# Tiles kept over the seams of attention, preparation and mixing, and q computed by tokens

## The chip, the cores and the metric

The kernel runs on one core of one Trainium2 chip. The metric is the device time of one execution in microseconds (us); several executions are given with their median. The core has five engines that run their own instruction queues: TensorE (PE in the rows, PEld its weight loads), VectorE (DVE), ScalarE (ACT), GpSimd (POOL) and SyncE (SP), which here issues nearly all DMA transfers. They wait for each other by semaphores.

## The reference

Four sequences of 512 tokens and 512 channels go through four residual layers. The change lies in the first (cross attention, 16 heads of 128, RMS norm on q and k) and at the start of the two that follow it in the kernel:

```python
q = (hidden_states @ Wq).reshape(B, Sq, H, D)
k = (encoder_hidden_states @ Wk).reshape(B, Skv, H, D)
v = (encoder_hidden_states @ Wv).reshape(B, Skv, H, D)
q = rmsnorm(q, gq)
k = rmsnorm(k, gk)
scores = jnp.einsum('bqhd,bkhd->bhqk', q, k) * scale
attn = jax.nn.softmax(scores, axis=-1)
out = jnp.einsum('bhqk,bkhd->bqhd', attn, v).reshape(B, Sq, H * D)
return out @ Wo

x = x + attention(layernorm(x), ctx_1024, ...)
x = x + hadamard_ffn(layernorm(x), ...)      # fwht, gate and up, silu(gate) * up, fwht, down
x = x + ssm(ctx_1024, layernorm(x), ...)     # in_proj, convolution, silu, low rank, softplus, scan
x = x + mixture_of_experts(layernorm(x), ...)
```

## The kernel before

It is written engine by engine: each stage is a block in which every engine has its own program, and what is written there is the order in which it runs. A `Scope` ends with a barrier of all engines and gives its tiles back. Matrix products are made of pairs of rounded parts: `split_product` gives three products, high x high, high x low and low x high (L99 to L101); so every result that is used in a product again is copied as its high part by ScalarE and subtracted as its low part by VectorE.

**Attention** (`stage_attention`) runs 32 iterations: 8 pairs of heads, hp, times 4 sequences, b; i = 4 hp + b, j = i + 1. Work of iteration i (scores, exp, transposed probabilities, attention product, projection) is woven with K, q and V of iteration j. Banks of PSUM: `ps_s` (scores), `ps_pt` (transposed probabilities), `ps_w` (three banks for K, q, V and the projection), `ps_o` (the attention product). K is computed by tokens, 128 at a time, for both heads (256 columns), copied to `kn`, squared by GpSimd, summed and scaled per token, and turned by transposes against the identity (`turn_k`, L365). q is computed by channels, already turned: `queries`, 12 products of 512 columns for each head. ScalarE makes its high part (L550) and its square (L551, `qsq`); the sum over the channels lies across partitions, so `sums_q` makes it with 8 products of `qsq` and a column of ones into `ps_o` (L371); GpSimd raises the result to -1/2 (L680), and `exp` takes it as a scale. On TensorE, the second half of an iteration reads: the first head's attention product, `turn_k` for both heads, `turn_p(1, 0)` and `turn_p(1, 1)` (L385, transposed probabilities of the second head), V's first half (`kv`), `turn_p(1, 2)`, `sums_q`, `turn_p(1, 3)`, V's second half, then the second head's attention product `pv(i, 1)`, which waits for VectorE's subtraction behind `turn_p(1, 3)` (L801). On VectorE: L781 (q low), L806 (the attention product's low part), L786 (K low), L801, L797 (q sums), L801. ScalarE splits a half of an expert's weights (L577) once per iteration; SP loads the context, expert weights, xn and ffn weights ahead.

**Preparation** (`stage_prep`): loads the in-projection, constants and the first context tiles, turns the in-projection (L1170) and the down weights (L1137), normalizes and turns four rows of x (`norm`, `turn`, `norm_out`), with the standard deviation by three Newton steps on VectorE. Then 16 steps of channel products (`channels`), a convolution of four taps on VectorE (L1437, L1440), rotation of the down weights, step sizes. GpSimd does the butterflies.

**Mixing** (`stage_mix`): 64 blocks, in which TensorE makes gate, up and down products and VectorE and GpSimd run the state recurrence: drive (L1918), decay (L1772, ScalarE), scan (L1989). SP loads delta, du, rows and, through three buffers, gate and up weights `gu` of 1 MB per block.

## Time and profile before

| | us |
|---|---|
| median of 3 runs | 2483.26 (2483.11 to 2485.51) |
| profiled execution | 2479.53 |
| its span | 2477.7 |
| TensorE busy | 2260.7 |
| VectorE busy | 1768.8 |
| GpSimd busy | 1366.2 |
| ScalarE busy | 1291.6 |

The span is the time from the first to the last instruction of the program that was profiled. Attention runs to about 1212 us, preparation to about 1351, mixing to about 2060, router and experts to the end. Busy times are unions over instructions; a TensorE row's duration is longer than its share, since products overlap: the distance of two starts tells what one costs. An idle time before an instruction is shown in brackets with what ended it; short ones are left out.

### The profile page before, as it was taken

What the parts mean: (1) busy time and instruction counts of PE and PEld (TensorE: products, weight loads), DVE (VectorE), ACT (ScalarE), POOL (GpSimd) and SP (SyncE); (2) the same over time, 40 slices, a digit from 0 to 9 for tenths busy, and PEclk for the clock granted to TensorE, in tenths of its full rate; (3) what the DMA queues carried; (4) which work ended last, traced back from release to release, by engine and by line L of the source; (5) the groups of instructions that cost most, each with busy time, mean ns of one, the idle gap of its engine ahead of it and who ended that gap; (6) DMA issues with size and microseconds to landing.
All of it is one profiled execution on the core that took longest, in us unless ns stands there. A gap on an engine that the chain in (4) does not pass through costs nothing. (4 is left out here: it accounts for less than half of the span.)

```text
span 2477.7 us, 31987 instructions
## 1 busy us (share of the span) xinstructions
PE 2260.7 (91%) x10784; PEld 1745.7 (70%) x10784; DVE 1768.8 (71%) x3390; ACT 1291.6 (52%) x2246; POOL 1366.2 (55%) x1107
## 2 busy tenths in 40 slices
PE   5899999999999999999695899899899986999994
PEld 4788888888888888888551666566566554777773
DVE  7676776777677676766585898898898996634344
ACT  3555555554555555555475766766766653223331
POOL 2444444444444444444185887997998993233331
PEclk9999999999999999999897999999999997899997
DMA  7655555464645545452446766565565532369865
GB/s 298 239 192 197 183 183 200 154 217 170 218 161 194 193 172 206 158 204 107 161 139 232 250 190 208 166 209 180 174 206 176 188 107 89 120 225 347 335 216 194
DMA packets 148066, 480.77 MB, mean 194 GB/s; under 512 B 24577, under 2 KB 61697, under 8 KB 124481
## 3 DMA queue, kind: packets, MB, share of 16 engines
q1 hardware_dynamic: 138208, 449.78, 51.7%
q0 software_dynamic: 7520, 24.74, 2.8%
q10 hardware_dynamic: 2176, 4.19, 0.4%
q8 instruction: 90, 1.47, 0.2%
q14 instruction: 72, 0.58, 0.1%
HBM read 361.19 MB, written 117.47 MB: 193 GB/s over the span
## 5 line engine op out<-in xcount | busy, mean ns | idle before, releaser
L671 POOL TENSOR_SCALAR att_probs<-att_probs,att_recip 128x512 f32<-128x512 f32 x256 | 179.2, 703 | 377.3 <-DVE att_recip L765 377.3
L1918 POOL TENSOR_TENSOR mix_drive<-mix_du,mix_rows 128x512 f32<-128x512 f32 x256 | 326.5, 1282 | 36.8 <-DMA mix_rows<-bc_d 9.4
L1989 DVE TENSOR_TENSOR_SCAN mix_state<-mix_state,mix_drive 128x512 f32<-128x512 f32 x256 | 312.9, 1222 | 42.4 <-POOL mix_drive L1918 30.1
L563 ACT ACTIVATE att_probs<-att_s,att_bias,att_rq 128x512 f32<-128x512 f32 x256 | 199.9, 781 | 226.9 <-DVE att_bias L761 226.6
L1772 ACT ACTIVATE mix_state<-mix_delta,mix_a 128x512 f32<-128x512 f32 x256 | 175.9, 690 | 217.8 <-DVE mix_drive L2000 188.0
L1903 POOL TENSOR_TENSOR mix_y<-mix_y,mix_drive 128x512 f32<-128x512 f32 x180 | 230.7, 1282 | 46.5 <-DVE mix_drive L2000 46.3
L1682 PE MATMUL mix_down<-mix_wd,mix_hT 128*128 128x512 f32 x512 | 233.9, 600 | 7.7 <-DVE residual_x L2020 7.7
L569 ACT CAST att_pT<-att_pt 128x512 fp32r<-128x512 f32 x256 | 143.6, 591 | 174.1 <-PE att_pt L385 169.5
L760 DVE TENSOR_REDUCE att_nmax<-att_s 128x1 f32<-128x512 f32 x256 | 174.8, 683 | 62.8 <-PE att_s L101 62.7
L801 DVE TENSOR_TENSOR att_pT<-att_pt,att_pT 128x512 fp32r<-128x512 f32 x256 | 170.1, 685 | 65.0 <-ACT att_pT L569 58.3
L1682 PEld LDWEIGHTS mix_down<-mix_wd,mix_hT 128*128 128x128 f32 x512 | 98.1, 192 | 110.1 <-issue 96.1
L99 PE MATMUL att_w<-att_w_qkv,att_cx 128*128 128x256 f32 x512 | 155.5, 304 | 0.2 <-POOL att_w_qkv L707 0.2
L385 PE MATMUL att_pt<-att_ident,att_probs 128*128 128x128 f32 x1024 | 141.8, 276 | 10.9 <-DVE att_pT L801 5.9
L101 PE MATMUL att_w<-att_w_qkv,att_cx 128*128 128x256 f32 x512 | 150.6, 294 | 0.0
L100 PE MATMUL att_w<-att_w_qkv,att_cx 128*128 128x256 f32 x512 | 150.4, 294 | 0.0
L680 POOL TENSOR_TENSOR att_rq<-att_qss,att_power 128x8 f32<-128x8 f32 x32 | 55.1, 1723 | 165.6 <-DVE att_qss L797 165.6
L697 POOL TENSOR_TENSOR att_expert_w<-att_expert_w 128x1536 fp32r<-128x1536 f32 x32 | 112.1, 3502 | 61.5 <-DVE att_w_qkv L747 34.2
L385 PEld LDWEIGHTS att_pt<-att_ident,att_probs 128*128 128x128 f32 x1024 | 118.2, 143 | 27.0 <-DVE att_pT L801 17.1
L2704 POOL DMA_INDIRECT parts<-exp_y,exp_target x47 | 49.2, 1048 | 152.9 <-ACT exp_y L2741 86.4
L2000 DVE TENSOR_TENSOR mix_drive<-mix_state,mix_rows 128x512 f32<-128x512 f32 x180 | 124.4, 691 | 6.2
L806 DVE TENSOR_TENSOR att_oT<-att_o,att_oT 128x512 fp32r<-128x512 f32 x64 | 44.2, 691 | 103.1 <-ACT att_oT L581 102.9
L812 DVE TENSOR_TENSOR residual_x<-att_w,residual_x 128x512 f32<-128x512 f32 x128 | 85.3, 686 | 37.1 <-PE att_w L101 37.1
(384 smaller groups left out, 6670.8 us busy)
## 6 DMA issues: line engine op xcount, KB each, us to landing
mix_gu<-guT SPq DMA_DIRECT2D x64, 1024.0 KB, 8.3
att_xn<-normT SPq DMA_DIRECT2D x31, 2048.0 KB, 8.6
split_w<-att_expert_w SPq DMA_DIRECT2D x32, 1536.0 KB, 6.4
lead_w<-split_w SPq DMA_DIRECT2D x16, 3072.0 KB, 12.1
mix_rows<-bc_d SPq DMA_DIRECT2D x128, 256.0 KB, 5.0
att_cx<-ctxT SPq DMA_DIRECT2D x30, 1024.0 KB, 8.6
guT<-att_ffnT SPq DMA_DIRECT2D x32, 512.0 KB, 6.1
mix_wd<-wdT SPq DMA_DIRECT2D x16, 1024.0 KB, 7.9
```

The source lines that it names most:

```text
L99: pe.matmul(out, lh, rh, start=start, stop=False)
L101: return pe.matmul(out, ll, rh, start=False, stop=stop)
L385: tr = pe.transpose(ps_pt[(b + n) % 2][:, t, :], probs[:, h * TB + t, k * P:(k + 1) * P], ident_sb[:, :])
L563: act.activation(probs[:, n, :], ps_s[n % 2][:, :], ACT.Exp, bias=bias[:, n:n + 1], scale=rq[:, n:n + 1], accum_out=sums[:, n:n + 1]).then ...
L671: pool.tensor_scalar(probs[:, n, :], probs[:, n, :], recip[:, n:n + 1], 1.0, ALU.mult, ALU.mult).then_inc(s_pn, 1)
L760: own.after(dve.tensor_reduce(nmax[:, n:n + 1], ps_s[n % 2][:, :], AX_X, ALU.max, negate=True))
L801: dve.tensor_tensor(pT[:, 1, k, :], ps_pt[(b + (TB + 1) * h + k) % 2][:, :, :].rearrange("p t n -> p (t n)"), pT[:, 0, k, :].bitcast(F32), ...
L1682: mm = pe.matmul(ps_y[:, :], hT[c % 2][:, k, tok], wd[c % 2][:, k, :], start=(k == 0), stop=(k == CHUNK - 1))
L1772: act.activation(state[q % BANKS][:, :], delta[i % DELTAS][:, :], ACT.Exp, scale=a[:, t, n:n + 1]).then_inc(s_decay, 1)
L1903: pool.tensor_tensor(out[:, :], out[:, :], drive[q % RING][:, :], ALU.add).then_inc(s_padd, 1)
L1918: pool.tensor_tensor(drive[q % RING][:, :], du[i % DUS][:, :], rows[g % ROWS][:, 0, :], ALU.mult).then_inc(s_drive, 1)
L1989: dve.tensor_tensor_scan(h[:, :], h[:, :], drive[q % RING][:, :], 0.0, ALU.mult, ALU.add).then_inc(s_scan, 1)
```

## The change

**q by tokens.** `queries` now works like `kv`: 128 tokens at a time, both heads, 256 columns, 48 products in place of 24. ScalarE copies q to a new tile `qn`, GpSimd squares it (`square_q`, in K's tile of squares), VectorE sums it (`sum_q`, now a reduction of 1024 elements per partition and a small one), and TensorE turns it (`turn_q`, 8 transposes) into the banks it came from; ScalarE and VectorE then make the parts. `sums_q`, the column of ones and the squares on ScalarE are gone.

```diff
+                def queries(half, bank):
+                    for a in range(2):
+                        t = 2 * half + a
+                        rows = slice(t * P, (t + 1) * P)
+                        for k in range(KD):
+                            mm = split_product(pe, ps_w[bank][:, a * W2:(a + 1) * W2],
+                                               (xn[:, 0, k, rows], xn[:, 1, k, rows]),
+                                               (wpart(0, "q", k), wpart(1, "q", k)), k == 0, k == KD - 1)
                     mm.then_inc(s_q, 1)
+
+                def turn_q(j, h, bank):
+                    pe.wait_ge(s_qc, 2 * j + 2)
+                    for t in range(TB):
+                        tr = pe.transpose(ps_w[bank][:, t * P:(t + 1) * P], qn[:, t, h, :], ident_sb[:, :])
+                    tr.then_inc(s_qt, 1)
...
                         turn_k(0, 1)
-                        pe.wait_ge(s_qlo, 2 * j + 1)
-                        turn_k(1, 2)
+                        turn_q(j, 0, 2)
                     turn_p(i, b, 1, 0)
                     turn_p(i, b, 1, 1)
                     if not last:
+                        turn_q(j, 1, 0)
+                        pe.wait_ge(s_qlo, 2 * j + 1)
+                        turn_k(1, 2)
+                    turn_p(i, b, 1, 2)
+                    if not last:
                         pe.wait_ge(s_qlo, 2 * j + 2)
                         kv(cx, "v", 0, 0, s_v)
-                    turn_p(i, b, 1, 2)
-                    pe.wait_ge(s_olo, 2 * i + 3)
-                    if not last:
-                        pe.wait_ge(s_qsq, 2 * j + 2)
-                        sums_q()
                     turn_p(i, b, 1, 3)
                     if not last:
                         pe.wait_ge(s_ktlo, 2 * j + 1)
                         kv(cx, "v", 1, 1, s_v)
-                        pe.wait_ge(s_qss, j + 1)
+                    pe.wait_ge(s_olo, 2 * i + 3)
                     pv(i, 1)
...
+                def square_q(j):
+                    pool.wait_ge(s_qc, 2 * j + 2)
+                    pool.wait_ge(s_kss, j + 1)
+                    pool.tensor_tensor(ksq[:, :, :, :], qn[:, :, :, :], qn[:, :, :, :], ALU.mult).then_inc(s_qsq, 1)
...
+                def sum_q(own, j):
+                    dve.wait_ge(s_qsq, j + 1)
+                    own.after(dve.tensor_reduce(qss[:, :], ksq[:, :, :, :].rearrange("p t h d -> p h t d"), AX_X, ALU.add))
+                    dve.tensor_scalar(qss[:, :], qss[:, :], 1.0 / D, RMS_EPS, ALU.mult, ALU.add).then_inc(s_qss, 1)
```

**Tiles over the seams.** A class `Bridge` takes the place of `Scales` and is allocated before attention. It holds the identity and Hadamard matrices, all small constants of preparation and mixing, a tile `raw` (attention's raw weights, then the in-projection, later the turned rows of mixing) and two tiles `gu`, which serve as context tiles in attention and preparation and then as the first two gate and up tiles of mixing.

```diff
+                    if b == B - 1 and 1 <= hp:
+                        for to, src in strided[hp - 1::PAIRS - 1]:
+                            sp.dma_start(to, src, allow_slow_non_contiguous=True).then_inc(s_strided, 16)
+                    if b == 1 and hp == PAIRS - 1:
+                        sp.wait_ge(s_w, 2 * PAIRS)
+                        sp.dma_start(raw[:, 0:ET * CD].rearrange("p (t d) -> p t d", t=ET),
+                                     in_proj.rearrange("(t p) d -> p t d", p=P)).then_inc(s_inproj, 16)
...
+                def load_gu(i):
+                    sp.wait_ge(s_x, ET * (B - 1 + i))
+                    sp.dma_start(bridge.gu[i][:, :, :, :, :].bitcast(F32), guT[i]).then_inc(s_gu, 16)
...
                 load_rows(0)
-                load_gu(0)
                 for i in range(1, ET):
                     load_delta(i)
                     load_du(i)
-                load_gu(1)
                 load_rows(1)
```

In preparation the in-projection, the identity and the first two contexts are there at the start; `norm`, `turn` and `norm_out` of the four rows move into the first four steps of the loop; GpSimd's power replaces the Newton steps; the signed Hadamard matrices (8 instructions, L1412 and L1413) move from the start to just ahead of the first convolution, and the statistics behind the scaling of the down weights:

```diff
+                input_lo(0)
+                input_lo(1)
+                dve.wait_ge(s_dsc, 1)
+                scale_down(0)
                 spread()
...
+                down_lo(0)
+                shifts()
+                down_lo(1)
                 signed_hadamard()
...
+                    if s < TB:
+                        norm(s)
                     if s < B * ET:
                         u(s // ET, s % ET)
```

How the order moves. TensorE in the second half of an attention iteration, before (kn is K by tokens, probs the probabilities, w_qkv with cx the V products):

```order
L365 MATMUL att_w<-att_ident,att_kn 128x128 x8
L385 MATMUL att_pt<-att_ident,att_probs 128x128 x8
L99 MATMUL att_w<-att_w_qkv,att_cx 128x256
...
L385 MATMUL att_pt<-att_ident,att_probs 128x128 x4
L371 MATMUL att_o<-att_ones,att_qsq 128x1 x8
```

and in the change, at the same place:

```order
L369 MATMUL att_w<-bridge_ident,att_kn 128x128 x4
L364 MATMUL att_w<-bridge_ident,att_qn 128x128 x4
L383 MATMUL att_pt<-bridge_ident,att_probs 128x128 x8
L364 MATMUL att_w<-bridge_ident,att_qn 128x128 x4
L369 MATMUL att_w<-bridge_ident,att_kn 128x128 x4
L383 MATMUL att_pt<-bridge_ident,att_probs 128x128 x4
L99 MATMUL att_w<-att_w_qkv,bridge_gu 128x256
```

The V products now stand behind seven groups of four transposes, and the products with ones are gone.

VectorE at the same place, before (oT is the attention product's low part, pT the probabilities' low part):

```order
L776 TENSOR_SCALAR att_kn<-att_kn,att_rk 128x128 x8
L781 TENSOR_TENSOR att_qT<-att_w,att_qT 128x512
L806 TENSOR_TENSOR att_oT<-att_o,att_oT 128x512
L786 SCALAR_TENSOR_TENSOR att_kT<-att_w,att_gain,att_kT 128x512 x2
L801 TENSOR_TENSOR att_pT<-att_pt,att_pT 128x512 x3
L797 TENSOR_SCALAR att_qss<-att_o 128x8
```

and in the change:

```order
L791 TENSOR_SCALAR att_kn<-att_kn,att_rk 128x128 x8
L822 TENSOR_TENSOR att_oT<-att_o,att_oT 128x512
L801 SCALAR_TENSOR_TENSOR att_kT<-att_w,att_gain,att_kT 128x512
L796 TENSOR_TENSOR att_qT<-att_w,att_qT 128x512
L817 TENSOR_TENSOR att_pT<-att_pt,att_pT 128x512 x2
L796 TENSOR_TENSOR att_qT<-att_w,att_qT 128x512
L801 SCALAR_TENSOR_TENSOR att_kT<-att_w,att_gain,att_kT 128x512
L812 TENSOR_REDUCE att_qss<-att_ksq 128x8
```

Both subtractions of q and the reduction of its squares now stand behind the attention product's.

## Rows read from the trace of the kernel before

**Rows 1.** Stretches (attention, mixing): us, busy PE, PEld, DVE, ACT, POOL, PEclk, DMA, GB/s.
```profile
77.00:1212.00 1135.00, 1115.84 (x6364) 956.47 (x6364) 799.25 (x1767) 597.58 (x1192) 508.36 (x437) 0.98 0.50 181
...
1363.00:2045.00 682.00, 634.06 (x2216) 413.88 (x2216) 609.96 (x720) 448.88 (x615) 606.99 (x485) 0.98 0.57 187
```

**Rows 2.** L577 up to 1180 us: count, duration ns min/median/max, first and last start.
```profile
L577 ACT CAST att_expert_w<-att_expert_w x31: 1474/1477/1484, 94.0 to 1169.4; 128x1536 fp32r<-128x1536 f32 x31
```

**Rows 3.** Timeline of TensorE in one iteration: start us, us, engine, line, op, count.
```profile
625.51 1.03 PE L365 MATMUL att_w<-att_ident,att_kn 128*128 128x128 f32 x8
...
628.99 0.66 PE L385 MATMUL att_pt<-att_ident,att_probs 128*128 128x128 f32 x4
629.49 1.84 PE L371 MATMUL att_o<-att_ones,att_qsq 128*128 128x1 f32 x16
631.19 0.64 PE L385 MATMUL att_pt<-att_ident,att_probs 128*128 128x128 f32 x4
...
633.32 0.48 PE L99 MATMUL att_o<-att_pT,att_v 128*128 128x512 f32 x1
...
660.92 1.04 PE L365 MATMUL att_w<-att_ident,att_kn 128*128 128x128 f32 x8
```

**Rows 4.** Timeline of VectorE in the same iteration, with the idle time before.
```profile
616.05 1.22 DVE L769 TENSOR_REDUCE att_kss<-att_ksq 128x8 f32<-128x1024 f32 x1 [1.18 <-POOL att_ksq L667]
...
626.33 0.69 DVE L806 TENSOR_TENSOR att_oT<-att_o,att_oT 128x512 fp32r<-128x512 f32 x1 [0.36 <-ACT att_oT L581]
626.94 1.40 DVE L786 SCALAR_TENSOR_TENSOR att_kT<-att_w,att_gain,att_kT 128x512 fp32r<-128x512 f32 x2
628.26 1.28 DVE L801 TENSOR_TENSOR att_pT<-att_pt,att_pT 128x512 fp32r<-128x512 f32 x2
...
632.48 0.69 DVE L801 TENSOR_TENSOR att_pT<-att_pt,att_pT 128x512 fp32r<-128x512 f32 x1 [0.95 <-ACT att_pT L569]
```

**Rows 5.** Timeline of ScalarE, the copy of the last transposed probabilities.
```profile
631.86 0.59 ACT L569 CAST att_pT<-att_pt 128x512 fp32r<-128x512 f32 x1 [1.59 <-PE att_pt L385]
```

**Rows 6.** Timeline of TensorE: twelve products of 256 columns, then twelve of 512.
```profile
609.27 0.28 PE L99 MATMUL att_w<-att_w_qkv,att_cx 128*128 128x256 f32 x1
...
610.73 0.50 PE L99 MATMUL att_s<-att_kT,att_qT 128*128 128x512 f32 x1
...
613.67 0.39 PE L99 MATMUL att_w<-att_xn,att_w_qkv 128*128 128x512 f32 x1
...
616.39 1.03 PE L385 MATMUL att_pt<-att_ident,att_probs 128*128 128x128 f32 x8
```

**Rows 7.** Timeline of TensorE, an iteration in which the clock falls.
```profile
1166.59 1.84 PE L371 MATMUL att_o<-att_ones,att_qsq 128*128 128x1 f32 x16
...
1169.03 0.41 PE L101 MATMUL att_w<-att_w_qkv,att_cx 128*128 128x256 f32 x1
```

**Rows 8.** Timelines of VectorE, then TensorE, at the start of the preparation stage.
```profile
1213.15 2.47 DVE L1395 BATCH_NORM_STATS2 prep_stats<-residual_x 128x6 f32<-128x512 f32 x4 [1.31 <-PEq L75]
...
1219.28 0.28 DVE L1412 TENSOR_SCALAR first_hs<-prep_had_f,prep_su 128x128 f32<-128x128 f32 x1
...
1221.97 1.28 DVE L1407 TENSOR_SCALAR prep_wraw<-prep_wraw,prep_dsc 128x2048 f32<-128x2048 f32 x1
...
1235.11 0.75 DVE L1437 TENSOR_SCALAR prep_conv<-prep_x,prep_taps 128x512 f32<-128x512 f32 x1 [0.47 <-PE prep_x L101]
...
1216.73 1.11 PE L1170 MATMUL prep_dbl_ps<-first_ident,prep_relu 128*128 128x128 f32 x4 [5.62 <-DMA first_ident<-in_ident]
...
1232.95 0.78 PE L99 MATMUL prep_x<-prep_cx,prep_inT 128*128 128x512 f32 x1
```

**Rows 9.** Timelines of GpSimd, TensorE and VectorE at the start of the mixing stage.
```profile
1360.70 1.26 POOL L1918 TENSOR_TENSOR mix_drive<-mix_du,mix_rows 128x512 f32<-128x512 f32 x1 [9.41 <-DMA mix_rows<-bc_d]
...
1363.31 0.80 PE L99 MATMUL mix_gate<-first_uT,mix_gu 128*128 128x512 f32 x1 [25.93 <-DMA mix_gu<-guT]
...
1370.76 1.23 DVE L1989 TENSOR_TENSOR_SCAN mix_state<-mix_state,mix_drive 128x512 f32<-128x512 f32 x1 [2.76 <-ACT mix_state L1772]
```

More of the change, by code:

```diff
@@ L101, in split_product, with stage_attention @@
     return pe.matmul(out, ll, rh, start=False, stop=stop)
[L104 to L119 removed]
+def stage_attention(nc, xs, x, ctx, xT, ctxT, Wq, Wk, Wv, Wo, gq, gk, W_gate, W_up, guT, Wg, Wu, Wd, split_w, ident, in_proj, bridge, strided):
     D = P
@@ L331, in _ @@
                 sp.wait_ge(s_est, 16 * PAIRS * B)
+                sp.wait_ge(s_strided, 16 * len(strided))
+                sp.wait_ge(s_inproj, 16)
+                for i in range(2):
+                    sp.wait_ge(s_cx[i], 16 * PAIRS * B // 2)
                 sp.wait_ge(s_fst, 16 * (PAIRS * B + 1))
@@ L366, in turn_k @@
                     tr.then_inc(s_kt, 1)
-                def sums_q():
-                    for n in range(HP * TB):
-                        h, t = divmod(n, TB)
-                        mm = pe.matmul(ps_o[:, n:n + 1], qsq[:, h, t * P:(t + 1) * P], ones[:, :], start=True, stop=True)
-                    mm.then_inc(s_ss, 1)
                 def turn_p(i, b, h, k):
@@ L648, in iteration @@
                         kt_hi(j, 0)
+                        q_hi(j, 0)
+                    pt_hi(i, b, 1, 0)
+                    pt_hi(i, b, 1, 1)
+                    if not last:
+                        q_hi(j, 1)
                         kt_hi(j, 1)
-                    for k in range(TB):
-                        pt_hi(i, b, 1, k)
+                    pt_hi(i, b, 1, 2)
+                    pt_hi(i, b, 1, 3)
                     expert_hi(i)
@@ L734, in iteration @@
                     norm_p(i, 7)
+                    if not last:
+                        square_q(j)
                     split_ffn(i)
@@ L908, in iteration @@
                     pt_lo(i, b, 0, 3)
-                    if not last:
-                        q_lo(j, 0)
                     row_recip(i, 7)
@@ L1493, with stage_mix @@
 EXPERTS = 16
[L1496 to L1498 removed]
+def stage_mix(nc, xs, uT0, hs, guT, wdT, bridge, u_d, delta_d, du_d, bc_d):
+    BLOCKS = bridge.sud.shape[1]
     ALL = B * BLOCKS
```

244 lines of the change are left out of this document (106 added, 138 removed).

## Prediction

> **What bounds the kernel now.** I read the stretches by stage first, then the timeline of one attention iteration on each engine, then the two seams. The attention stage fills nearly half of the span, and in it TensorE is busy 1115.8 of 1135 us; no other engine is above 800 us [rows 1]. So the stage lasts as long as TensorE's row of work plus its waits. The reader is to see in [rows 2] that 31 L577 starts, one per iteration, lie between 94.0 and 1169.4 us: 35.85 us each. An iteration in which nothing disturbs the clock is shorter: from one first L365 to the next, 660.92 - 625.51 = 35.41 us [rows 3]. The rest, 30 x 0.44 = 13 us, is the clock: in some iterations, right behind the one-column products of L371, TensorE goes from 2.4 to 1.2 GHz: the 256-column product takes 0.41 us there and 0.28 elsewhere [rows 6, 7], and the stage's granted clock is 0.98 [rows 1]. Such an iteration is 1.1 to 1.2 us longer, so there are about 12 of them.
>
> The stretch that the change rewrites runs from L365 (start of the K transposes, 625.51) to the second head's attention product (633.32): 7.81 us [rows 3]. Call its start 0. In it TensorE already waits: twice, for 0.2 to 0.3 us, for VectorE's subtractions. VectorE is the chain behind it: L806 at 0.82, two L786 from 1.43, two L801 from 2.75 to 4.03, and the last L801 at 6.97 [rows 4].
>
> The mixing stage is the second long one: TensorE 634 of 682 us, VectorE 610, GpSimd 607 [rows 1]. They are coupled in the order of the blocks, so it moves as a whole with its start.
>
> **The change part by part. First, q by tokens.**
> (1) Removed on TensorE: 8 one-column products per iteration, L371 from 629.49 to the next row at 631.19, 1.70 us [rows 3].
> (2) Added on TensorE: 8 transposes of q. Eight K transposes take 0.87 us [the start of row L365 in rows 3 to the next group], or 0.1 us each; so 0.8 us.
> (3) Changed: 24 products of 512 columns become 48 of 256. Twelve of the first kind last 616.39 - 613.67 = 2.72 us, so 0.227 each; twelve of the second 610.73 - 609.27 = 1.46, so 0.12 each [rows 6]. 48 x 0.12 - 24 x 0.227 = +0.3 us. It lies in a part of the iteration where TensorE waits for nobody, so it counts in full.
> By work alone this would be -1.70 + 0.8 + 0.3 = -0.6 us per iteration.
>
> (4) But TensorE gets three new places to wait at, all on VectorE. I walk through the stretch. TensorE now has K head 0, q head 0, two groups of probabilities, q head 1: 20 transposes, done at 2.05. The next row (K head 1) writes the bank of q head 0, and waits for its subtraction. VectorE now does L806 at 0.82, one K subtraction at 1.43 (0.66), the q subtraction at 2.09 (same shape as L806, 0.69 long), done at 2.78 [durations from rows 4]. TensorE waits some 0.8 us. Then VectorE has two probability subtractions (0.6 each) and q head 1's, done at 2.69 + 3 x 0.61 + 0.1 = 4.6. The first half of the V products writes that bank, so it starts at 4.7, not at 1.7 as now; behind it in TensorE's queue stands the last transpose of probabilities. 12 x 0.12 plus 0.08 for the switch puts that at 6.22; now it is at 5.68 (631.19) [rows 3]. From there to the attention product it is ScalarE's copy 0.67 later, VectorE's subtraction 0.62 after that, its 0.69 and 0.15 more: 2.13 us [rows 3 to 5]. So the product starts at 8.35 in place of 7.81: **+0.54 us**. In that time VectorE also has the K head 1 subtraction (0.66) and the new sum of q squares: a reduction of 1024 elements per partition, like L769's 1.22 us, plus a small one [rows 4]. It is free at 7.14 and is needed at 7.5, so it hides, with 0.36 us to spare.
> Bounds of this term. Below: VectorE's rows of the new stretch add up to 7.0 us back to back (0.61 x 6 + 0.66 x 2 + 1.34 + 0.69), from 0.82; the product can't start before 7.95, so it is at least +0.14. Above: each of the three waits may bring 0.1 us of wake-up more, and the reduction may outlast its cover by 0.3: +0.85. I take 0.54, since every step has a row of the same shape. All that comes behind the attention product is TensorE's row, so it passes the loss on.
> (5) ScalarE loses two squarings and gets no more than it loses; GpSimd gets a square of 1024 elements behind its last normalization, in a gap before the ffn split. ScalarE and GpSimd are busy 598 and 508 of 1135 us [rows 1], so at nothing; if it weren't covered, GpSimd's 1.9 us would delay the q sum and show in (4).
> (6) SP: ten small strided loads and in_proj's go before the expert load, one or two per pair of heads, and two context loads at the end. Expert halves and xn have most of an iteration; at nothing.
> So an iteration gets longer by 0.54 + 0.3 = 0.84, and 31 have it: **+26 us** (bounds 0.44 and 1.15: +14 and +36).
>
> (7) The clock. With the ones products the known cause of the falls is gone. But from 0 to 4.7 TensorE now does nothing but 28 transposes and waits; today the longest run without a wide product goes from 628.99 to the four transposes at 631.19 and their 0.4 us, 2.6 us [rows 3]. I put the falls at 16 instead of 12, **+5 us**; bounds: none left (-13) and one in every iteration (+23).
> The Trainium skill (TensorE: Matmul & The Clock Gate, "Why this matters for your kernels") wants only that the engine has no long idle gaps between bursts; the falls in [rows 7] come without any, so here row and rule differ. By that rule neither version would fall, and the sum would be 13 us lower. Part 4 of the same page, on PE-mode transposes, says that these do not count as busy for the clock; by it the new stretch of transposes is worse than today's, which is the last rival below.
>
> **Second, the seam from attention to preparation.** Now the stage begins at 1213.15 (VectorE); TensorE waits until 1216.73 for the identity matrix, turns weights and the first normed rows by turns, and comes to the first channel product at 1232.95; the first convolution starts at 1235.11 [rows 8]. With matrices resident, I walk it anew from 1213.2 at the same low clock: turn 1.1, copy 0.6, subtract 0.7, twice: 1218.1. VectorE scales the down weights (1.28 us [rows 8]; their load now stands first in the queue, and I take it as landed by 1218.5) until 1219.8. VectorE then has the statistics, 2.47 us [rows 8] and 0.7 for small ones, before its subtraction, which ends at 1223.6. Two rotations of 512 columns (0.43 each at 1.2 GHz) and a turn (0.9) put the first channel product at 1225.4, 7.5 us earlier. Behind it the signed Hadamard, 8 instructions 0.2 us apart (0.28 each [rows 8]), now stands just ahead of the first convolution: 1228.7, **-6.4 us**. The normalizations of four rows and their turns go into the loop, into ScalarE's and TensorE's idle time; not covered, they would cost 4 x 1 us. Bounds -3 and -8. VectorE's convolutions pace the stage, so its end moves along.
>
> **Third, the seam to mixing.** GpSimd starts at 1360.70 on the rows, TensorE at 1363.31 on gate weights; they and the second block's (1 MB each) stand in the load queue between the first chunk's rows and the other chunks. The third scan on VectorE, 1370.76, waits 2.76 us for ScalarE [rows 9], whose decay stands in its order behind the sigmoid of that late gate. With both weight blocks there, gate and up of block 0 are done before the rows come, and du and delta 1 have 1 MB less ahead of them (5.6 us at the stage's 187 GB/s [rows 1]; I take 4, since a burst runs above a mean). The third scan goes from 1370.76 to about 1365: **-5.8 us**. Bounds -3 (only the queue's part) and -9 (the rows come earlier too).
>
> **Sum**: +26 + 5 - 6.4 - 5.8 = **+19 us** on the profiled execution's 2479.5, 2498.5; the median of the runs is 3.7 above that execution, so 2502.
>
> **The rivals.**
> A. *Faster, the walk is wrong and TensorE's work decides*: if the three waits do not arise, (1) to (3) give 31 x -0.6 = -18, the seams -12, the falls up to -13: 2440 to 2453. For it: TensorE is busy 98% of the stage. Against: VectorE's own 7.0 us don't fit into a stretch of 7.2. It decides from where the q subtractions end before 2.1 and 3.5. Chance 0.12.
> B. *The falls vanish with the ones products*, the walk holds: 26 - 13 - 12 = +1, 2484. Chance 0.17.
> C. *Waits at their lower bound or seams at their upper*: 14 + 5 - 17 = +2, down to -10 with fewer falls: 2473 to 2486. Chance 0.13.
> D. *The clock falls in each iteration*: +26 + 23 - 12 = +37, 2520. For it: 4.7 us with transposes only. Chance 0.15.
> E. *The seams don't pay* (the loads just come late elsewhere, the rows pace the mix's start as before): +31, 2514. Chance 0.05.
> My forecast, with falls between 8 and 22, has 0.38, and reaches from 2490 to 2514.
>
> **How the numbers follow.** The time is the forecast's, 2502. The range has it with B, C, D and E for the most part: 2470 to 2522; A is left out. A measurement of this kernel can tell about 0.2%, 5 us. Faster by more: A, a third of C and of B: 0.22. Within: the rest of these two, 0.15. Slower: 0.63.
>
> **What would show it.** In the profile after: L371 gone; TensorE's wait for the q subtraction (VectorE) ahead of the K head 1 turn, about 0.8 us, and another of 0.8 ahead of the first V product; 8.3 to 8.4 us from the K turn to the attention product; L577's successor 36.2 us apart in an undisturbed iteration, and 37.4 where the clock fell. The first channel product some 12 us behind the stage's start (now 20), the third scan of mixing some 14 us behind its start (now 19.6). It would be wrong if iterations came out at 34.8, or if granted clock in attention went to 1.00 or under 0.95 (now 0.98 [rows 1]).

## The result, and the profile after

The changed kernel takes **2547.61 us** (median of 4 runs, 2541.56 to 2548.3), the kernel before 2483.35 us in runs beside it (2483.11 to 2485.51). The ratio is 1.0251, 95% interval 1.0236 to 1.0266: 64 us slower, where I had forecast 19 slower and a range that ended at 2522. The profiled execution took 2547.45 us, its span is 2544.8.

First the stretches of the profile after that answer to [rows 1] (columns as there), attention and then mixing:

```profile
77.00:1287.00 1210.00, 1115.61 (x6847) 972.89 (x6844) 912.75 (x1796) 607.96 (x1190) 565.24 (x469) 0.98 0.48 171
1421.00:2105.00 684.00, 634.04 (x2205) 413.81 (x2206) 607.53 (x717) 451.40 (x619) 603.23 (x483) 0.97 0.57 187
```

Mixing is as it was. Attention is 75 us longer and TensorE's busy time in it the same 1116 us, so what came in is waiting. VectorE, with 29 instructions more, is busy 113 us more. That is too much for 31 sums of 1.4 us (43 us); the rest lies in one line of the program, the scaling of K, below. The expert copies of ScalarE, one per iteration, answer to [rows 2]; they are now (1243.5 - 93.8) / 30 = 38.32 us apart, and 38.10 where nothing disturbs the clock:

```profile
L575 ACT CAST att_expert_w<-att_expert_w x31: 1475/1480/1486, 93.8 to 1243.5; 128x1536 fp32r<-128x1536 f32 x31
```

Next, what TensorE waited for in attention (us in total, times, longest), after and then before, where the view's longest entries are single events:

```profile
PE att_w L369 <- DVE att_kn L791: 55.3, 29, 1.9
PE att_w L99 <- DVE att_qT L796: 12.2, 23, 0.6
PE att_w L369 <- DVE att_qT L796: 7.1, 17, 0.4
```
```profile
PE att_pt L385 <- DVE att_pT L801: 3.2, 2, 2.1
PE att_s L99 <- ACT att_probs L563: 1.3, 1, 1.3
```

The two waits for q (L796) are the ones that I had forecast. The one at the top is not in my sum at all: the turn of K head 0 waits 1.9 us for the scaling of K, which the change doesn't touch. Here are VectorE, GpSimd and TensorE in one iteration of after:

```profile
617.34 5.06 DVE L791 TENSOR_SCALAR att_kn<-att_kn,att_rk 128x128 f32<-128x128 f32 x8
...
617.52 0.76 POOL L683 TENSOR_SCALAR att_probs<-att_probs,att_recip 128x512 f32<-128x512 f32 x1 [0.41 <-DVE att_recip L780]
...
618.25 1.89 POOL L679 TENSOR_TENSOR att_ksq<-att_qn 128x1024 f32<-128x1024 f32 x1
...
620.12 0.61 POOL L698 TENSOR_SCALAR att_ffnT<-att_ffn_raw 128x512 fp32r<-128x512 f32 x1
...
620.81 1.30 POOL L700 TENSOR_TENSOR att_ffnT<-att_ffn_raw,att_ffnT 128x512 fp32r<-128x512 f32 x1
...
622.45 0.66 PE L369 MATMUL att_w<-bridge_ident,att_kn 128*128 128x128 f32 x4 [1.91 <-DVE att_kn L791]
```

VectorE's eight scalings take 5.06 us from start to end. Before, in the iteration of [rows 3], they took 2.36:

```profile
623.01 2.36 DVE L776 TENSOR_SCALAR att_kn<-att_kn,att_rk 128x128 f32<-128x128 f32 x8
```

One scaling is usually 0.28 us long. The view of the tile gives count, shortest, median and longest in ns, before and then after:

```profile
L776 DVE TENSOR_SCALAR att_kn<-att_kn,att_rk x256: 267/276/648, 39.2 to 1162.2; 128x128 f32<-128x128 f32 x128
```
```profile
L791 DVE TENSOR_SCALAR att_kn<-att_kn,att_rk x256: 267/282/1950, 39.4 to 1235.1; 128x128 f32<-128x128 f32 x128
```

The longest is 1.95 us, and GpSimd's new square beside it is 1.89 us. Laid beside GpSimd's rows, four of the eight are stretched: one of 0.64 us that runs until the last normalization ends, one of 1.95 beside the square, one of 0.67 beside the first half of the ffn split (0.61) and one of 1.28 beside its second half (1.30). GpSimd's instruction has begun first each time, and the stretched scaling ends some 0.08 us behind its end, in all 124 cases of this trace. Between the two halves of the split one scaling of the usual length gets through. So VectorE's instruction lasts as long as what is left of GpSimd's. The kernel before shows the same in small: its longest scaling, 648 ns against a median of 276, stands beside a normalization of 0.77, and in all 31 iterations one scaling is stretched so beside the normalization and one beside the first half of the split (0.67).

### The profile page after: what moved, and what is told of

Same layout as the page of the kernel before. It is cut to its first block and busy times, and to the rows that moved or that the text cites. A ratio compares the mean times of both kernels' runs of the same rounds, so it can differ in the third digit from the quotient of the medians.

```text
span 2544.8 us, 33092 instructions
## 1 busy us (share of the span) xinstructions
PE 2267.4 (89%) x11296; PEld 1766.2 (69%) x11296; DVE 1883.2 (74%) x3407; ACT 1302.7 (51%) x2246; POOL 1425.0 (56%) x1141
## 5 line engine op out<-in xcount | busy, mean ns | idle before, releaser
L99 PE MATMUL att_w<-att_w_qkv,bridge_gu 128*128 128x256 f32 x512 | 150.4, 294 | 13.1 <-DVE att_qT L796 12.8
L791 DVE TENSOR_SCALAR att_kn<-att_kn,att_rk 128x128 f32<-128x128 f32 x256 | 158.4, 691 | 0.2 <-POOL att_rk L688 0.2
L383 PE MATMUL att_pt<-bridge_ident,att_probs 128*128 128x128 f32 x1024 | 150.4, 289 | 2.2 <-DVE att_pT L817 1.1
L99 PE MATMUL att_w<-att_w_qkv,att_xn 128*128 128x256 f32 x512 | 148.0, 289 | 0.0
L100 PE MATMUL att_w<-att_w_qkv,att_xn 128*128 128x256 f32 x512 | 145.3, 284 | 0.0
L101 PE MATMUL att_w<-att_w_qkv,att_xn 128*128 128x256 f32 x512 | 145.3, 284 | 0.0
L100 PE MATMUL att_w<-att_w_qkv,bridge_gu 128*128 128x256 f32 x512 | 144.0, 281 | 0.0
L101 PE MATMUL att_w<-att_w_qkv,bridge_gu 128*128 128x256 f32 x512 | 143.9, 281 | 0.0
L2707 POOL DMA_INDIRECT parts<-exp_y,exp_target x47 | 49.3, 1048 | 152.8 <-ACT exp_y L2744 101.9
```

Source lines behind the costliest of these rows:

```text
L99: pe.matmul(out, lh, rh, start=start, stop=False)
L100: pe.matmul(out, lh, rl, start=False, stop=False)
L101: return pe.matmul(out, ll, rh, start=False, stop=stop)
```

## The experiments

**1. The square behind the scalings** (late_square), the changed kernel with one wait more. GpSimd works in the order of its program, so the split of the ffn piece moves behind the scalings too:

```diff
                 def square_q(j):
                     pool.wait_ge(s_qc, 2 * j + 2)
                     pool.wait_ge(s_kss, j + 1)
+                    pool.wait_ge(s_kn, j + 1)
```

> The changed kernel with one wait more: GpSimd's square of q starts only when VectorE's eight scalings of K are done. Theory (the two engines take turns at something both need): in the changed kernel one of the eight scalings of every iteration lasts 1,950 ns, as long as the square of 1,890 ns beside it, two more last 0.67 and 1.28 us beside GpSimd's split of the ffn piece (0.61 and 1.30 us), the eight take 5.06 us in place of 2.36, and TensorE waits 1.91 us for them. With the square behind the scalings, and the split behind the square, the eight should take about 2.0 us, TensorE's wait for them should be gone (at most 0.2 us), and the undisturbed iteration should fall from 38.1 to about 36.2 us: 31 x 1.9 = 59 us, so 2,547 - 59 = 2,488 us (2,480 to 2,500, by how often the granted clock falls). Rival (the scalings are late for another reason, say their order in VectorE's queue, and the long scaling only looks like the square's): the eight still take about 5 us and the time stays at 2,540 to 2,550. Second rival (what the square does beside the scalings it then does beside the K parts, the q parts or V): the eight are short, but VectorE's subtractions behind them become longer by as much, and less than 20 us come back.

Measured: 2477.06 us (10 runs, ratio to before 0.9968, interval 0.9954 to 0.9982), and 2477.68 (12 runs) when it ran once more below. 70 us are gone, more than I expected. The scalings, their longest, the square and TensorE's next row in its trace:

```profile
587.74 1.99 DVE L792 TENSOR_SCALAR att_kn<-att_kn,att_rk 128x128 f32<-128x128 f32 x8
...
589.91 1.89 POOL L680 TENSOR_TENSOR att_ksq<-att_qn 128x1024 f32<-128x1024 f32 x1 [1.23 <-DVE att_kn L792]
...
590.81 0.60 PE L369 MATMUL att_w<-bridge_ident,att_kn 128*128 128x128 f32 x4
...
592.48 1.28 POOL L701 TENSOR_TENSOR att_ffnT<-att_ffn_raw,att_ffnT 128x512 fp32r<-128x512 f32 x1
...
592.89 0.68 DVE L797 TENSOR_TENSOR att_qT<-att_w,att_qT 128x512 fp32r<-128x512 f32 x1
```

1.99 us for the eight, no wait on TensorE. And the subtractions that now stand beside GpSimd's work, as the last row, are no longer than elsewhere (0.68 us); one of their operands lies in PSUM. So the second rival falls too. Between two L575 starts an undisturbed iteration is 36.03 us in place of 38.10: 31 x 2.07 = 64 us. The other 7 are the clock (experiment 7).

**2. The same work, needless, in the kernel before** (spare_square), where GpSimd squares the K squares in place once more:

```diff
+                def square_again():
+                    pool.tensor_tensor(ksq[:, :, :, :], ksq[:, :, :, :], ksq[:, :, :, :], ALU.mult)
...
                     norm_p(i, 7)
+                    if not last:
+                        square_again()
                     split_ffn(i)
```

> The kernel before with one instruction more in each iteration and nothing else changed: GpSimd squares the 1,024 elements of the K squares once more, in place, at the spot where the change puts the square of q (behind the eighth normalization, ahead of the split of the ffn piece). Nobody reads the result and nobody waits for it. Theory: the eight scalings of K go from 2.36 to about 5 us as in the changed kernel, TensorE's K turns start 2.0 to 2.6 us later, and with them the iteration is 37.4 to 38.0 us in place of 35.4: 31 x (2.0 to 2.6) = 62 to 81 us, so 2,545 to 2,564 us. Rival (an idle GpSimd does this work free, as the prediction had it): 2,483 to 2,490 us, scalings at 2.36.

Measured: 2577.26 us, ratio 1.0374 (1.0357 to 1.0391): 93 us for an instruction nobody waits for.

```profile
627.08 5.06 DVE L781 TENSOR_SCALAR att_kn<-att_kn,att_rk 128x128 f32<-128x128 f32 x8
...
627.99 1.90 POOL L670 TENSOR_TENSOR att_ksq<-att_ksq 128x1024 f32<-128x1024 f32 x1
...
632.20 1.11 PE L365 MATMUL att_w<-att_ident,att_kn 128*128 128x128 f32 x4 [2.47 <-DVE att_kn L781]
```

The 5.06 us to the hundredth. The undisturbed iteration is 38.01 us, 2.60 longer than before, so 81 us, the end of what I expected; the time lies above it. The profiled execution was 2561.73 us, 78 over the median of before; the other four, at a mean granted clock of 0.948 to 0.951 against its 0.955, were 9 to 18 us longer. That more falls of the clock make up this rest is argued, not shown.

**3. The control** (spare_late), the same spare square started behind the scalings:

```diff
                     if not last:
+                        pool.wait_ge(s_kn, j + 1)
                         square_again()
```

> The control for the spare square: the kernel before with the same needless GpSimd square of 1,024 elements in every iteration, but started only when VectorE's eight scalings of K are done. The amount of work on every engine is that of the run with the spare square, only its place differs. Theory (place, not amount: the two engines take turns only where both work from and to SBUF): the eight scalings take about 2.0 us, TensorE waits for none of them, 2,483 to 2,490 us. Rival (the iteration is longer because GpSimd has 1.9 us more work, wherever it lies): 2,540 us or more.

Measured: 2487.14 us, ratio 1.0008 (0.9989 to 1.0027), no difference. The scalings take 2.00 us, and TensorE's K turns have no wait before them:

```profile
626.02 2.00 DVE L782 TENSOR_SCALAR att_kn<-att_kn,att_rk 128x128 f32<-128x128 f32 x8
...
628.10 1.90 POOL L670 TENSOR_TENSOR att_ksq<-att_ksq 128x1024 f32<-128x1024 f32 x1 [1.14 <-DVE att_kn L782]
...
628.46 1.04 PE L365 MATMUL att_w<-att_ident,att_kn 128*128 128x128 f32 x8
```

Its square starts 2.08 us behind the first scaling's start (628.10 against 626.02), in the run before 0.91 (627.99 against 627.08). GpSimd's 1.9 us more per iteration cost nothing in the one place and 93 us in the other, 1.2 us earlier. It is the place.

**4. Half the square** (half_square); the sums for half of the tokens of q are left wrong:

```diff
-                    pool.tensor_tensor(ksq[:, :, :, :], qn[:, :, :, :], qn[:, :, :, :], ALU.mult)
+                    pool.tensor_tensor(ksq[:, 0:2, :, :], qn[:, 0:2, :, :], qn[:, 0:2, :, :], ALU.mult)
```

> The changed kernel, but GpSimd squares only the first half of q (512 of 1,024 elements a partition; the sums of the other half are left wrong, so the output isn't the reference's). Nothing else is changed. Theory: one scaling of K lasts as long as the square beside it, so with a square of about 0.95 to 1.0 us in place of 1.89 the longest of the eight should last about 1.0 us in place of 1.95, the eight about 4.1 in place of 5.06, and the iteration should be 0.9 us shorter: 31 x 0.9 = 28 us, 2,519 us (2,512 to 2,526). Rival (a fixed cost of every change of engine, whatever the length): the same 2,547 within 4 us. Rival (the scalings are only slowed in proportion while both run): also less than the full 0.9 us, 2,530 to 2,540.

Measured: 2510.31 us, ratio 1.0104 (1.0084 to 1.0125), 37 us less than the changed kernel.

```profile
639.43 4.22 DVE L791 TENSOR_SCALAR att_kn<-att_kn,att_rk 128x128 f32<-128x128 f32 x8
...
640.34 1.03 POOL L679 TENSOR_TENSOR att_ksq<-att_qn 128x512 f32<-128x512 f32 x1
...
643.71 0.66 PE L369 MATMUL att_w<-bridge_ident,att_kn 128*128 128x128 f32 x4 [1.06 <-DVE att_kn L791]
```

The square is 0.86 us shorter, the eight scalings 0.84, TensorE's wait 0.85, the iteration 0.86 (37.24). One for one: neither a fixed cost for each meeting nor a mere slowing in proportion. 31 x 0.86 = 27; of the other 10 us some 7 are the clock, which no longer falls in the loop (experiment 7), and the rest stays open.

**5. The square on ScalarE** (scalar_square):

```diff
                     ffn_out(i, b)
+                    if not last:
+                        act.wait_ge(s_qc, 2 * j + 2)
+                        act.wait_ge(s_kss, j + 1)
+                        act.activation(ksq[:, :, :, :], qn[:, :, :, :], ACT.Square).then_inc(s_qsq, 1)
```

> The changed kernel with the square of q on ScalarE, one Square of 1,024 elements from the SBUF copy, put in ScalarE's idle 2.1 us between its copy of the ffn piece and its copy of the attention product; no wait is added. GpSimd does as much as before the change. Theory: ScalarE beside the scalings costs them nothing, but GpSimd's split of the ffn piece (0.61 and 1.30 us) still falls among them, so the eight take about 3.7 us (2.0 + 0.4 + 1.3), TensorE waits 0 to 0.5 us for them, and the iteration is 36.0 to 36.6 us: 2,474 to 2,492 us. Rival (the scalings suffer from any other engine that reads SBUF): 5 us again and 2,540 us or more.

Measured: 2488.15 us, ratio 1.0013 (0.9995 to 1.0031). ScalarE reads and writes the same tiles as GpSimd did, beside the same scalings:

```profile
627.40 3.39 DVE L791 TENSOR_SCALAR att_kn<-att_kn,att_rk 128x128 f32<-128x128 f32 x8
```
```profile
628.42 1.07 ACT L550 ACTIVATE att_ksq<-att_qn 128x1024 f32<-128x1024 f32 x1
...
628.62 0.67 POOL L701 TENSOR_SCALAR att_ffnT<-att_ffn_raw 128x512 fp32r<-128x512 f32 x1 [0.28 <-ACT att_ffn_raw L576]
...
629.37 1.33 POOL L703 TENSOR_TENSOR att_ffnT<-att_ffn_raw,att_ffnT 128x512 fp32r<-128x512 f32 x1
```

The longest scaling here is 1.31 us, as GpSimd's last row, and GpSimd's two rows explain the whole: what the eight take over the 1.99 of late_square, 1.4 us, is less than the two (0.67 + 1.33), and nothing is left for ScalarE's 1.07. TensorE waits 0.24 us for the scalings, and the iteration is 36.43: 31 x 0.40 = 12 us over late_square, where 11 were measured. This also parts the 2.07 us of experiment 1: 38.10 - 36.43 = 1.67 us per iteration are the square, the other 0.40 the two rows of the split that stay beside the scalings here.

**6. The seams alone** (seams_only), the q part undone:

> The changed kernel with the q part undone: q, its squares and its sums by products with ones as in the kernel before, and only the tiles kept over the seams (weights, transposed context, gate and up weights, identity, the small vectors) with the new order of the preparation. In the changed kernel the stretch from the start of the preparation to the end is about 7.3 us shorter than before. Theory (the two halves of the change are independent): attention takes as long as before, and the total is 2,483 - 7 = 2,476 us (2,471 to 2,480). The prediction had 12 us for this half: 2,471. Rival (the kept tiles or the loads put among the last iterations of attention cost something there): 2,480 to 2,490, with longer iterations where the loads stand.

Measured: 2477.25 us, ratio 0.9971 (0.9955 to 0.9986): 7 us faster, 4 to 11. Attention is as before (its stage ends at the same 1213). So the q part by itself costs some 71 us, and the seams give 7 back. Preparation starts with (TensorE and VectorE of after, answering to [rows 8]):

```profile
1287.58 0.63 PE L1179 MATMUL prep_dbl_ps<-bridge_ident,bridge_raw 128*128 128x128 f32 x4 [2.05 <-PEq L75]
...
1299.76 0.78 PE L99 MATMUL prep_x<-bridge_gu,prep_inT 128*128 128x512 f32 x1
```
```profile
1293.04 1.29 DVE L1415 TENSOR_SCALAR prep_wraw<-prep_wraw,prep_dsc 128x2048 f32<-128x2048 f32 x1 [1.42 <-DMA prep_wraw<-in_L_ffn_W_down]
...
1302.93 0.74 DVE L1442 TENSOR_SCALAR prep_conv<-prep_x,bridge_taps 128x512 f32<-128x512 f32 x1
```

The first channel product comes 12.2 us behind the stage's start (19.8 before), the first convolution 15.4 (22.0 before). The third scan of mixing, and what it waits for:

```profile
1436.73 1.23 DVE L1992 TENSOR_TENSOR_SCAN mix_state<-mix_state,mix_drive 128x512 f32<-128x512 f32 x1 [0.75 <-ACT mix_state L1775]
```

**7. The products with ones, put back as a load** (ones_back), on top of late_square; what they write is read by nobody. They are 8 products, which the trace shows as 16 rows:

```diff
+                def sums_again():
+                    for n in range(HP * TB):
+                        h, t = divmod(n, TB)
+                        pe.matmul(ps_o[:, n:n + 1], qn[:, t, h, :], ones[:, :], start=True, stop=True)
...
+                    pe.wait_ge(s_olo, 2 * i + 3)
+                    if not last:
+                        sums_again()
                     turn_p(i, b, 1, 3)
```

> The changed kernel with the square behind the scalings, and the 16 one-column products per iteration put back on TensorE as a load only, ahead of the last turn of P (they multiply the copy of q by a column of ones; what they write is overwritten and read by nobody). In the run with the late square the granted clock falls in no iteration of attention (none between 89 and 1205 us), in the kernel before in 12 of 31, behind those products. Theory 1 (the products bring the falls): 16 x 115 ns = 1.84 us more per iteration, and the clock falls again in 8 iterations or more, at about 1.2 us each: 31 x 1.84 = 57, plus 10 to 15, 2,544 to 2,550 us. Theory 2 (the falls come with TensorE's waits or with the phase of the iteration only): 1.84 us more and no fall, 2,530 to 2,538 us. What both leave open: how much of the 1.84 us hides behind the wait for the second q head; then 5 to 10 us less in both.

Measured: 2527.03 us, ratio 1.017 (1.0132 to 1.0208), 3 us under the range of theory 2. The iteration is 37.73 to 37.83 us, 1.70 to 1.80 more than 36.03. And the clock does not fall: the whole middle of attention at full clock, as in late_square, against 0.98 in the kernel before. The stretch from 90 to 1180 us in before, in late_square and in this run (columns as in [rows 1]):

```profile
90.00:1180.00 1090.00, 1082.48 (x6191) 930.64 (x6192) 770.46 (x1706) 576.54 (x1150) 494.06 (x422) 0.98 0.51 184
```
```profile
90.00:1180.00 1090.00, 1055.19 (x6647) 923.65 (x6646) 783.14 (x1729) 578.37 (x1145) 548.30 (x452) 1.00 0.52 184
```
```profile
90.00:1180.00 1090.00, 1059.32 (x6813) 930.04 (x6812) 750.95 (x1659) 552.05 (x1094) 519.38 (x433) 1.00 0.50 177
```

So the one-column products by themselves don't bring the falls, though they stand ahead of them in [rows 7]. They aren't cleared altogether: all 37 falls between 90 and 1180 us in before, seams_only and spare_late come from 0.3 us before to 0.9 us behind the end of these products, and there four transposes stand right ahead of them (2.6 us without a wide product), which this run doesn't put back (2.1 us). A run with both was not made. In the changed kernel 13 of 30 iterations are longer than 38.15 us, by 0.5 us on the mean; each of the 13 falls comes 0.2 to 1.3 us behind the end of the long wait. There the turns behind the wait of 1.91 us run at 1.2 GHz, 1.06 us for four where another iteration takes 0.60:

```profile
698.63 0.66 PE L369 MATMUL att_w<-bridge_ident,att_kn 128*128 128x128 f32 x4 [1.91 <-DVE att_kn L791]
...
701.01 1.06 PE L364 MATMUL att_w<-bridge_ident,att_qn 128*128 128x128 f32 x4
701.87 1.06 PE L369 MATMUL att_w<-bridge_ident,att_kn 128*128 128x128 f32 x4
```

With the order of the change and no wait over 1.1 us (late_square, half_square, scalar_square, ones_back) there is no fall between 90 and 1180 us. A long wait alone doesn't decide it either: order_late below waits 1.79 us in each of 30 iterations and falls in two of them. With the order of before (before, seams_only, spare_late) the clock falls 10 to 15 times in this stretch, which has one wait of over 2 us at most. What in that order brings them stays open.

**8. Another order on TensorE** (order_late), on top of late_square:

```diff
                         turn_q(j, 1, 0)
+                        pe.wait_ge(s_ktlo, 2 * j + 1)
+                        kv(cx, "v", 0, 1, s_v)
                         pe.wait_ge(s_qlo, 2 * j + 1)
                         turn_k(1, 2)
...
                     if not last:
                         pe.wait_ge(s_qlo, 2 * j + 2)
-                        kv(cx, "v", 0, 0, s_v)
+                        kv(cx, "v", 1, 0, s_v)
                     turn_p(i, b, 1, 3)
-                    if not last:
-                        pe.wait_ge(s_ktlo, 2 * j + 1)
-                        kv(cx, "v", 1, 1, s_v)
```

The two halves of V so change banks; their copies, their subtractions and the projection's waits follow.

> The changed kernel with the square behind the scalings and another order on TensorE: the first half of V goes into the bank that the first K head leaves (bank 1), ahead of the second K turn, and the second half into bank 0, so that neither waits for the subtraction of q. In the run with the late square TensorE waited 0.47 us (30 times) for the first q head and 0.5 us (31 times) for the second. Theory: both waits go, nothing takes their place (the first K head's subtraction ends at 592.98 there, 0.1 us before the second q turn's end at 593.16), the iteration falls from 36.03 to 35.0 to 35.2 us: 31 x 0.9 = 28 us, 2,449 us (2,440 to 2,458). Rival (the next wait stands just behind: TensorE gets to the turns of P or to the second attention product before ScalarE and VectorE have left them): less than 10 us, 2,467 to 2,477. Second rival (a denser stretch makes the granted clock fall again, as in 12 iterations of the kernel before, at 1.2 us each): 2,455 to 2,470.

Measured: 2488.53 us, ratio 1.0014 (0.9998 to 1.003), 11 us worse than late_square: the first rival, and more. The iteration is 36.30 us, 0.27 longer, and two iterations with a fall of the clock are 1.3 and 1.6 longer still. Both waits went, and this one came:

```profile
601.32 1.21 DVE L810 TENSOR_REDUCE att_qss<-att_ksq 128x8 f32<-128x1024 f32 x1
...
602.64 1.28 DVE L815 TENSOR_TENSOR att_pT<-att_pt,att_pT 128x512 fp32r<-128x512 f32 x2
...
604.07 0.47 PE L99 MATMUL att_o<-att_pT,att_v 128*128 128x512 f32 x1 [1.79 <-DVE att_pT L815]
```

The attention product now waits for two subtractions of P, which stand behind the sum of q's squares on VectorE. My expectation had checked only the wait next in line.

**9. The order on all three engines** (order_both), on top of order_late; VectorE's part is shown, and ScalarE and TensorE alike take piece 2 of P ahead of K head 1, TensorE also piece 3 ahead of the second half of V:

```diff
                     if not last:
                         q_lo(j, 1)
-                        kt_lo(j, 1)
-                        sum_q(own, j)
                     pt_lo(i, b, 1, 2)
+                    if not last:
+                        kt_lo(j, 1)
                     pt_lo(i, b, 1, 3)
+                    if not last:
+                        sum_q(own, j)
```

> The run with the other order (order_late) traded its two waits of 0.5 us for one of 1.79 us: TensorE's second attention product waited for VectorE's last subtraction of P (604.07 there), because VectorE stood 1.38 us at the sums of q's squares (601.32 to 602.73) and TensorE had turned the last piece of P only behind both halves of V. This run moves three things on top: TensorE turns the third piece of P ahead of the second K head and the fourth ahead of the second half of V, ScalarE and VectorE take them in that order, and VectorE's sums of q come behind the last subtraction of P (rq is then ready about 4 us before the first maximum asks for it). Theory: the last subtraction of P ends about 0.2 us after TensorE's second half of V, the wait shrinks from 1.79 to 0 to 0.4 us, and the iteration from 36.30 to 34.5 to 34.9 us: 31 x 1.6 = 50 us, 2,488 - 50 = 2,438 us (2,430 to 2,450), 45 us under the kernel before. Rival (another wait stands just behind, for the subtraction of q, for a bank of V or in the next iteration's K products): 35.3 to 36 us, 2,458 to 2,480. Rival (the granted clock falls again once the iteration has changed): 10 to 20 us of the gain are lost, 2,448 to 2,460.

Measured: **2447.15 us**, ratio 0.9849 (0.9832 to 0.9865): 37 us faster than the kernel before and 100 faster than the change.

```profile
582.64 0.68 DVE L817 TENSOR_TENSOR att_pT<-att_pt,att_pT 128x512 fp32r<-128x512 f32 x1
...
583.24 1.21 DVE L812 TENSOR_REDUCE att_qss<-att_ksq 128x8 f32<-128x1024 f32 x1
...
583.47 0.47 PE L99 MATMUL att_o<-att_pT,att_v 128*128 128x512 f32 x1 [0.51 <-DVE att_pT L817]
```

The iteration is 34.90 us, in seven of 30 36.0: there VectorE splits the next pair's weights ahead of the second attention product's subtraction, and TensorE waits 1.2 us for it. From the K turn to the attention product it is 7.1 us, where before it is 7.81 [rows 3].

**10. One seam undone** (late_square_again, mix_loads_back): the first two blocks of gate and up weights loaded in mixing again.

> The kernel of the run late_square once more, as the partner of the next one on the same chip; the difference of the two is what is asked. 2,477 us, 2,472 to 2,481.

> The kernel of late_square with the mixing seam undone: the first two blocks of gate and up weights are loaded at the start of mixing, as in the kernel before, and no longer during the preparation; everything else stays. The prediction gave this seam 5.8 us (bounds 3 and 9), the run with the seams alone gave both together 7.2 us (3.5 to 11) in place of the 12.2 forecast. Theory 1 (the mixing seam is worth what the start of the third scan moves, and the stage keeps it): the third scan starts 4 to 6 us later from the stage's start, and the run is 4 to 6 us longer than late_square, 2,481 to 2,483. Theory 2 (the later part of mixing waits for something else and gives it back): the third scan moves but the total by less than 2 us, 2,477 to 2,479; then the 7 us of both seams come from the preparation alone.

Measured: 2477.68 us (ratio 0.997, 0.9959 to 0.9981) and 2479.67 (0.9987, 0.9977 to 0.9997), 12 runs each: 2 us by the medians, 4 by the ratios, and the intervals overlap. The third scan starts in the one and in the other at

```profile
1364.14 1.23 DVE L1993 TENSOR_TENSOR_SCAN mix_state<-mix_state,mix_drive 128x512 f32<-128x512 f32 x1 [0.38 <-ACT mix_state L1776]
```
```profile
1368.90 1.23 DVE L1991 TENSOR_TENSOR_SCAN mix_state<-mix_state,mix_drive 128x512 f32<-128x512 f32 x1 [2.96 <-ACT mix_state L1774]
```

that is 148.6 and 152.8 us behind the first transpose of preparation (1215.59 and 1216.09): 4.3 us. The scan moves as theory 1 has it, with the wait for ScalarE back (2.96 us, 2.76 in [rows 9]); how much of it the stage keeps, 2 us or 4, these runs can't tell.

## Why the prediction was wrong, point by point

- **The failed step is (5)**: "GpSimd gets a square of 1024 elements behind its last normalization, in a gap before the ffn split ... so at nothing". I asked whether GpSimd had time for it (508 busy of 1135 us [rows 1]), and not what runs on the other engines in that gap. VectorE's scaling of K does, on the path to TensorE. The step priced the wrong thing even in its hedge: it named the q sum as what would be late, and that one had 7 us to spare (the square ends at 620.14, its reduction starts at 627.58). It measured 2.07 us per iteration, 64 us in all (experiment 1), 1.67 of them the square and 0.40 the split beside the same scalings (experiment 5), and no rival and no bound had it. The row that could have told me was there: a scaling of 648 ns with a median of 276 in the kernel before, in every iteration, next to GpSimd.
- The Trainium skill states the mechanism (SBUF — State Buffer, "SBUF: two separate sides" and "Who interferes with whom"): VectorE and GpSimd share a pair of SBUF ports, taken exclusively for a whole instruction; tensor_scalar from SBUF to SBUF can take it, a tensor_reduce never does, and ScalarE has its own. The runs agree: the longest scaling is 1.95 us beside a square of 1.89 and 1.10 beside the half square of 1.03, and nothing is lost beside ScalarE's 1.07. It says that the engine that starts second is blocked. The trace agrees: in all 124 stretched scalings GpSimd had begun first. GpSimd itself loses little, 0.76 us for a normalization among the scalings and 0.69 elsewhere. That it gets in ahead each time because eight short instructions leave places between them is my reading, not shown.
- **(1) to (3)**, TensorE's work, held in the main. The ones products cost 1.70 to 1.80 us put back (1.70 forecast). The transposes come at 0.12 us each (20 in 2.41 us, from 622.45 to 624.86) where I had 0.10. What late_square adds outside the stretch of (4) is 0.62 - 0.42 = 0.20 us, where (3) had 0.3.
- **(4)**, the walk through the stretch, held: 8.23 us from the K turn (622.45) to the attention product, and the same in late_square, where I had 8.35. The two waits for q are there, but 0.41 and 0.54 us long rather than 0.8: they end where VectorE's chain puts them, 2.82 and 4.61 us behind the K turn (2.8 and 4.7 forecast), and the longer transposes fill the rest. With the square out of the way the iteration is 36.03 - 35.41 = 0.62 us longer than before; the sum said 0.84. 31 x 0.62 = 19 us in place of 26.
- **(7)**, the clock, had the wrong sign: 13 iterations with a fall cost 7 us, where 12 had cost 13 [rows 2, 3]. The number of falls was near the 16 forecast; it is the price that was wrong, 0.5 us each in place of 1.1, and they came behind the wait that I had not seen. Its ground ("the known cause of the falls is gone", the products with ones) was shaken in experiment 7, and its other one, that transposes alone would bring them, fell: late_square has no fall behind its 28. The rule on idle gaps of the Trainium skill (TensorE: Matmul & The Clock Gate, "Why this matters for your kernels") covers neither order: the kernel before falls where TensorE hardly waits, and of two runs with waits of 1.8 to 1.9 us one falls in 13 of 30 iterations and the other in two.
- **The preparation seam** moved as walked at its start: 12.2 us to the channel product (12 forecast), the first convolution 6.6 earlier (6.4). But mixing starts only 4.1 us earlier (133.9 us behind the start of preparation, 138.05 before): the stage gave 2.5 back. **The mixing seam**: third scan 15.2 us behind the start (14 forecast, 19.6 before), 4.4 in place of 5.8. The two terms were 12.2 together and measured 7.
- (6), SP's loads, cost nothing: attention in seams_only ends where it did.
- Sum as measured: 19 for the walk, 64 for the square and the split beside the scalings, -6 for the clock, -7 for the seams, 70; by the profiled executions it is 68, by the medians 64.
- Rival B (no falls, 2484) would have been close, had the square been late: late_square is 2477.

## What to carry to other kernels

Before a step goes to an idle GpSimd, look at which VectorE instructions lie under it: if they are scalings from SBUF to SBUF and TensorE waits behind them, as here, nearly the step's whole length goes onto the path (1.67 us of 1.89), and a single wait that puts it beside reads from PSUM took it off again. The sign in a profile is one line whose longest instruction is far above its median, by the length of a GpSimd row beside it. And when an order of work is changed to take out a wait, move the instructions on all the engines that feed the next one, and check the second wait behind the first.

## What the runs showed of the hardware

- Eight scalings of 128 elements a partition, SBUF to SBUF, take 1.66 us with no GpSimd instruction beside them (the first group of each run), 1.99 us beside a single normalization, 2.36 beside one row of the ffn split too, 3.39 beside both, 4.22 with a GpSimd square of 1.03 us added and 5.06 with one of 1.89.
- VectorE's subtractions with one operand in PSUM and its reduction of 1024 elements have the same length beside GpSimd's work as elsewhere (0.68 and 1.22 us, within 0.02), and so has ScalarE's square (1.06 us in the one case with no scaling of VectorE beside it, at most 1.08 in the others).
- GpSimd loses little: its square is 1.89 us among the scalings and 1.89 behind them, its normalization 0.76 and 0.69.
- Eight one-column products on TensorE in each iteration, in the order of ones_back, leave its granted clock at 1.00. An order in which it waits 0.5 us twice keeps it there; with a wait of 1.9 us more the clock falls in 13 of 30 iterations, and with a single wait of 1.8 us (order_late) in two of 30.
